# One core, four layers of two transformers: a reordered FFN entry, first batch, softmax maxima and last tail

## The chip, the cores and the metric

The kernel runs on one core of a Trainium2 chip. Its engines each have a queue of their own and meet only through semaphores: TensorE (PE in the profile, its weight loads PEld), VectorE (DVE), ScalarE (ACT), GpSimd (POOL) and SyncE (SP), which issues most of the DMAs. The metric is the time of one execution on the device in microseconds, the median over several runs.

## The reference

Four layers are applied to `x` (4 batches of 512 rows x 512 columns), each added to its input; `ctx` is 4 x 512 x 128:

```python
x = x + L0_xattn(layernorm(x), ctx, ctx)  # RMS norm, rope, 16 query heads on 4 kv heads, causal softmax, w_out
x = x + L0_ffn(layernorm(x))     # silu(x Wg) * (x Wu) Wd, DFF 1376, each with shared and routed rank-8 terms
x = x + L1_xattn(layernorm(x), ctx)
x = x + L1_ffn(layernorm(x))     # 64 experts, top 8, capacity 128 in order of tokens, silu(x Wg) * (x Wu) Wd

def L1_xattn(p, k_v):
    kv = k_v @ W_k.T + b_k
    sim = (p @ kv) @ kv.T * 512 ** -0.5
    sim = (sim - mean(sim)) * rsqrt(var(sim) + 1e-6) * ln_gamma + ln_beta
    return softmax(sim)

def L1_ffn(x):      # T = 2048 tokens
    topk_w, topk_idx = top_k(softmax(x @ router_w.T), 8)
    pos = (cumsum(onehot(topk_idx), axis=0) * onehot).sum(-1) - 1     # place of a token in its expert
    ...             # gather by expert, three products, weighted scatter-add
```

## The kernel before, in words

**Stages.** The four batches run one after another, then all 64 experts. A batch (512 rows = 4 tiles `t` of 128) goes through the attention of layer 0 (`attention`, on every engine a function of that name), its output projection, and the first FFN (`ffn`) in 11 chunks of 128 hidden columns (`NF`). The second cross-attention of a batch and its router, its tail, runs beside the attention of the next batch (`tail` is true there); the tail of the last batch has nothing beside it and is written out alone (`last_tail`, `last_list`, `last_rows`). `keep_clock(bank, n)` issues n spare bf16 products of 512 columns whose result nobody reads. The order on each engine is that of the code; nothing reorders it but the DMA queues.

**Attention.** Four groups `g` of four heads. The scores of a group stand in PSUM in six units (`MAX_UNITS`: tile 3 in two, tile 2 in two, tile 1, tile 0). For each unit VectorE takes the negated row maxima (`maximum(g, i)`, L1446), ScalarE the exponentials with their sums (`exps`, L905), and TensorE turns the probabilities (`turn`, L2120) through three banks used in a ring; VectorE and ScalarE copy them out (`turned`). `stack(g + 1, n)` turns keys (0) and queries (1 to 4) of the next group through the same ring. `normalise(g - 1)` multiplies the last group's output by the inverse sums (L1479), after which GpSimd splits it into a rounded part and a rest (`split_output`). In batch 0 the queries of groups 1 to 3 are still to be made between these (`query_part`, L1310 and L1317, on VectorE).

**Start.** VectorE takes the statistics of the rows, GpSimd the inverse roots; then come keys (`first_keys`), the row shifts (`row_shifts`, fshift) for which ScalarE waits before it makes normed rows (L864), and queries.

**FFN.** Weights come as f32 by DMA (`WRAW`), are rounded to fp32r by ScalarE (`WHI`: `wg_hi`, `wd_hi`) and their rest taken by VectorE (`WLO`: `wg_rest`, `wd_rest`), so that each product is three products. `normed`, `turned`, `turned_rest` make, turn and split the normed rows. Chunk 0's down products (`down_first`, L2448, L2454) use `HH[0]`, `HL[0]`, the two parts of the hidden values, made by GpSimd (L722, L726). Tiles 0 and 1 of its sum go to the banks in which chunk 1's gate and up stood, so they wait for `hid_ready` of chunk 1.

**Last tail.** Output rows (`o1`), their spread under the covariance of the keys (`COV`), weighted (`qv_ready`), give the variance of each similarity row by a product with ones (L2564); GpSimd takes the roots (`power`, L682). `y` scales the similarities, `peak_y` takes maxima, ScalarE exponentials, `x3` the new rows; `top`, `chosen` pick 8 experts, `positions` their places in the lists (a product of the mask with a triangle of ones), to which `TAKEN`, the counts of the earlier batches, is added. `one_hots` writes the list as products of one-hot tiles, `last_slots` masks it (OWN) and `SPREAD_R` brings it into place; IDX then lets the first gather start.

## Time and profile before

| | |
|---|---|
| median of 3 runs | 1270.76 us (1270.14 to 1270.92) |
| profiled execution, whole | 1271.93 us |
| its span, first to last instruction | 1270.1 us |
| mean granted TensorE clock | 0.985 |
| PE busy | 1192.1 us (94%), 6589 products |
| DVE / ACT / POOL busy | 57% / 41% / 38% of the span |
| chain that ended last | PE 77%, DVE 9%, ACT 6%, issue 2%, POOL 2%, DMA 1% |

The span is cut by the profile into stages: the start to 25 us, attention of batch 0 to about 98, FFNs of about 107 us and attentions of about 100 us in turn, the last tail from 875, experts from 918 to 1235, and the last scatters. In a timeline row stand start and length in us, engine, line, operation, out<-in with shapes and count, and in brackets how long the engine had been idle before and what ended it. Starts of neighbouring rows on one engine lie closer than their lengths, since an engine begins an operation before the last is through. In a row of windows stand the stretch and its length, busy time (and instructions) of PE, PEld, DVE, ACT and POOL, the granted TensorE clock as a share of 2.4 GHz, and the DMA share and GB/s. A row of the waits says who waited for whom.

### The profile page before, as it was taken

The numbers are of one execution on the slowest core, as the hardware profiler recorded it, in microseconds if no ns is written. First come the engines' busy times: TensorE is split into PE (matmuls) and PEld (weight loads), VectorE is DVE, ScalarE is ACT, GpSimd is POOL, SyncE is SP. The second block draws the span as 40 slices with busy tenths as digits, with TensorE's granted clock in tenths as the row PEclk, the third lists the DMA queues.
The fourth block names the chain that finished last, engine by engine and source line by source line (L and its number), as shares of the span: only waits on it lengthen the run. The fifth ranks groups of instructions, "written<-read, shape, count | busy, mean of one in ns | idle before, by whom it ended". The sixth has DMA issues, their size and how long they took to land.

```text
span 1270.1 us, 19545 instructions
## 1 busy us (share of the span) xinstructions
PE 1192.1 (94%) x6589; PEld 864.8 (68%) x6589; DVE 724.8 (57%) x1476; ACT 525.2 (41%) x1198; POOL 488.3 (38%) x541
## 2 busy tenths in 40 slices
PE   7998999999999999999999999999899999999980
PEld 4667777667877766777776687777566666666650
DVE  7967565686778578687867866655622222222220
ACT  5864222786322278632247843222332333333220
POOL 1431243462233446123453702121355555565630
PEclk9999999999999999999999999999999999999995
DMA  8012231003233000423300023534789999999847
GB/s 298 4 70 76 103 110 63 2 1 123 90 140 106 33 1 12 148 101 104 128 1 1 34 104 141 217 104 170 256 284 348 353 346 352 354 351 356 205 60 142
DMA packets 45922, 187.04 MB, mean 147 GB/s; under 512 B 6732, under 2 KB 9804, under 8 KB 31380
## 3 DMA queue, kind: packets, MB, share of 16 engines
q1 hardware_dynamic: 30980, 146.18, 30.7%
q0 software_dynamic: 14864, 39.85, 13.7%
q8 instruction: 45, 0.74, 0.2%
q14 instruction: 33, 0.27, 0.1%
HBM read 155.31 MB, written 34.90 MB: 150 GB/s over the span
## 4 chain that ended last, share of the span: by engine, by line
PE 77%; DVE 9%; ACT 6%; issue 2%; POOL 2%; DMA 1%; SPq 0%; DVEq 0%; POOLq 0%; ACTq 0%
PE PS L2613 14%; PE PS L2030 11%; PE PS L2032 11%; PE PS L2031 11%; PE PS L2629 4%; PE PS L2120 3%; ACT P L905 3%; PE PS L2633 3%; PE PS L2139 3%; DVE NM L1446 2%; PE PS L2603 2%; PE PS L2049 2%; PE PS L2430 1%; PE PS L2431 1%; PE PS L2622 1%
## 5 line engine op out<-in xcount | busy, mean ns | idle before, releaser
L2613 PE MATMUL PS<-WE,XGT 128*128 128x384 f32 x512 | 192.7, 499 | 1.5 <-DVE HM L2004 0.8
L722 POOL CAST HH<-HID 128x512 fp32r<-128x512 f32 x44 | 37.5, 852 | 323.9 <-DVE HID L1832 323.9
L1034 ACT ACTIVATE WHI<-WRAW 128x1280 fp32r<-128x1280 f32 x44 | 56.0, 1272 | 244.1 <-DMA WRAW<-in_ffn 244.1
L2030 PE MATMUL PS<-XTH,WHI 128*128 128x512 f32 x352 | 140.7, 400 | 0.0
L905 ACT ACTIVATE P<-PS,NM 128x512 f32<-128x512 f32 (+3 forms) x256 | 131.7, 532 | 15.8 <-DVE NM L1446 15.7
L2032 PE MATMUL PS<-XTH,WLO 128*128 128x512 f32 x352 | 138.2, 393 | 0.0
L2031 PE MATMUL PS<-XTL,WHI 128*128 128x512 f32 x352 | 138.0, 392 | 0.0
L2613 PEld LDWEIGHTS PS<-WE,XGT 128*128 128x128 f32 x512 | 87.1, 190 | 56.7 <-issue 21.5
L2011 DVE COPY HMT<-PS 128x256 f32<-128x256 f32 x64 | 27.2, 425 | 163.9 <-PE PS L2622 163.9
L1446 DVE TENSOR_REDUCE NM<-PS 128x2 f32<-128x1024 f32 (+2 forms) x96 | 98.3, 1040 | 30.7 <-PE PS L2039 30.4
L2120 PE MATMUL PS<-ident,P 128*128 128x128 f32 x640 | 94.2, 279 | 11.8 <-ACT P L905 5.5
L2120 PEld LDWEIGHTS PS<-ident,P 128*128 128x128 f32 x640 | 70.3, 142 | 26.6 <-ACT P L905 16.4
L1176 ACT ACTIVATE SL<-PS 128x192 f32<-128x192 f32 x64 | 21.1, 330 | 152.5 <-PE PS L2613 152.5
L682 POOL TENSOR_TENSOR sm<-sm,mhalf 128x4 f32<-128x4 f32 (+1 forms) x20 | 18.4, 918 | 157.8 <-DVE sm L1365 152.7
L2032 PEld LDWEIGHTS PS<-XTH,WLO 128*128 128x128 f32 x352 | 66.2, 188 | 16.2
L2030 PEld LDWEIGHTS PS<-XTH,WHI 128*128 128x128 f32 x352 | 66.2, 188 | 14.4
L2031 PEld LDWEIGHTS PS<-XTL,WHI 128*128 128x128 f32 x352 | 66.3, 188 | 14.3
L809 POOL DMA_INDIRECT XG<-hx,IDX x56 | 56.4, 1007 | 44.3 <-POOL IDX L806 43.5
L2049 PE MATMUL PS<-KST,QST 128*128 128x512 f32 (+3 forms) x256 | 67.6, 368 | 3.8 <-ACT P L905 3.5
L726 POOL TENSOR_TENSOR HL<-HID,HH 128x512 fp32r<-128x512 f32 x44 | 68.9, 1566 | 3.5
L821 POOL DMA_INDIRECT out<-YE,IDX x32 | 51.0, 1594 | 50.0 <-DVE HM L2004 17.2
L821 POOL DMA_INDIRECT acc<-YE,IDX x32 | 50.8, 1588 | 50.2 <-DMA acc<-YE,IDX 15.9
(341 smaller groups left out, 2737.8 us busy)
## 6 DMA issues: line engine op xcount, KB each, us to landing
WE<-in_we SPq DMA_DIRECT2D x64, 1152.0 KB, 8.1
WRAW<-in_ffn SPq DMA_DIRECT2D x44, 1060.0 KB, 5.0
acc<-HN SPq DMA_DIRECT2D x17, 256.0 KB, 6.4
out<-X SPq DMA_DIRECT2D x4, 1024.0 KB, 4.9
out<-acc POOLq DMA_DIRECT2D x1, 4096.0 KB, 22.9
hx<-HN SPq DMA_DIRECT2D x3, 1152.0 KB, 4.5
XIN<-in_x SPq DMA_DIRECT2D x3, 1024.0 KB, 5.3
CTX<-in_ctx SPq DMA_DIRECT2D x4, 256.0 KB, 2.9
```

Of the source, the lines that this page charges most:

```text
L726: pool.tensor_tensor(HL[slot][:, :], HID[:, :], HH[slot][:, :], ALU.subtract).then_inc(S["hl_ready"], 1)
L809: pool.indirect_dma_start(out=XG[s][:, :], out_offset=None, in_=hx, in_offset=bass.IndirectOffsetOnAxis(ap=IDX1[s][:, 0:1], axis=0),).then ...
L821: pool.indirect_dma_start(out=(out, acc)[s % 2], out_offset=bass.IndirectOffsetOnAxis(ap=IDX1[s][:, 0:1], axis=0), in_=YE[s % NY][:, :], i ...
L905: act.activation(prob(t, n), PS[:, c0:c0 + (t + 1) * P], ACT.Exp, bias=NM[:, c:c + 1], accum_out=SSUM[:, c:c + 1]).then_inc(S["p_ready"], 1)
L1034: act.activation(WHI[slot][:, 0:WD], WRAW[slot][:, 0:WD], ACT.Copy).then_inc(S["wg_hi"], 1)
L1446: dve.tensor_reduce(NM[:, t * HPG + n0:t * HPG + n0 + nh], src, AX, ALU.max, negate=True).then_inc(S["s_max"], 1)
L2030: pe.matmul(dst, a[0], b_[0], start=first, stop=False, **kw)
L2031: pe.matmul(dst, a[0], b_[1], start=False, stop=False, **kw)
L2032: return pe.matmul(dst, a[1], b_[0], start=False, stop=last, **kw)
L2049: pe.matmul(PS[:, a:a + n_keys], QST[n0 + n][:, t * P:(t + 1) * P], KST[:, 0:n_keys], start=(a % 512 == 0), stop=False, skip_group_check=True)
L2120: mm = pe.transpose(bank(bk, c, c + P), prob(t, n0 + n)[:, j * P:(j + 1) * P], ident[:, :])
L2613: mm = pe.matmul(bank(2 + s % 2, 0, 2 * F1), XGT[s % 2][:, k, :], WE[s][:, k * 2 * F1:(k + 1) * 2 * F1], start=(k == 0), stop=(k == KC - 1))
```

## The change

It has ten parts, all in the order or the shape of work; one adds products, one drops spare ones.

1. FFN, every batch: in `down_first` the products with `HL[0]` for ranks and tiles 2 and 3 come ahead of the wait for chunk 1's hidden values.
2. FFN of batch 0: ScalarE makes the first normed rows ahead of key columns and weights, and turns tiles 0 and 1 out ahead of the next weights; VectorE splits both turned tiles before it takes the weights' rest.
3. Start: `row_shifts` comes ahead of the key products and of the wait for the tables; the last add of the other groups' keys (`key_rows`) comes after the first two maxima.
4. Attention, groups 2 and 3: the maximum of unit 4 is taken in two halves with `normalise` between; ScalarE waits for each half. In group 2 the keys are copied out ahead of the last maximum.
5. Batch 0: `query_part(g + 2, 0)` comes after the copy of tile 1's probabilities.
6. Batch 0: `context_T` comes ahead of the last `turn`.
7. Last tail: row variances, their roots and scales in two halves, the products for them in another order.
8. Last tail: `TAKEN` is put under the positions by TensorE (4 products more) and not added by VectorE.
9. Last list: spare products after tiles 1, 2 and 3 go (6 of 8).
10. Last list: OWN is written in two halves, and its products wait for each.

GpSimd's roots of the last tail, and ScalarE's exponentials:

```diff
-            for n in (3, 4, 5):
-                power(B - 1, n)
-            pool.wait_ge(S["norm_out"], 1 + NORMS * B)
+            power(B - 1, 3)
+            power(B - 1, 4, 0, 2)
+            power(B - 1, 5, 2, NT)
+            power(B - 1, 6)
+            pool.wait_ge(S["norm_out"], 1 + NORMS * B + 1)
...
-                act.wait_ge(S["s_max"], 1 + MU * gi + i + 1)
+                act.wait_ge(S["s_max"], 1 + MAXIMA * gi + (i + 2 if i > SPLIT_UNIT else i + 1))
                 for n in range(n0, n0 + nh):
+                    if i == SPLIT_UNIT and n == HPG // 2:
+                        act.wait_ge(S["s_max"], 1 + MAXIMA * gi + i + 2)
                     c0, c = at + (n - n0) * width, t * HPG + n
                     act.activation(prob(t, n), PS[:, c0:c0 + (t + 1) * P], ACT.Exp, bias=NM[:, c:c + 1],
```


ScalarE in `ffn`, where `key_columns` is the copy of KV, `first_weights` the wait for `op_ps` and `wg_hi(0)`, `weights_ahead` `wd_hi(0)` and `wg_hi(1)`:

```diff
+                if b > 0:
+                    key_columns(b)
+                    first_weights()
+                act.wait_ge(S["shift_ready"], 1 + 2 * b + 1)
+                normed(0)
+                normed(1)
+                if b > 0:
+                    weights_ahead()
+                else:
+                    key_columns(b)
+                    first_weights()
+                turned(0)
+                turned(1)
+                if b == 0:
+                    weights_ahead()
+                act.wait_ge(S["shift_ready"], 1 + 2 * b + 2)
+                normed(2)
+                normed(3)
```

VectorE, in this order the start (`key_rows` is the last add of the keys), the attention, the split of turned rows, the last list and the last tail:

```diff
                 assert fstep.n == FIRST["scaled"], fstep.n
+            row_shifts()
             dve.wait_ge(tables_loaded, TABLES_LOADED)
-            dve.wait_ge(S["f_out"], 1 + 1)
-            fstep(first_keys(0, HD, [XN[:, 3, i * P:(i + 1) * P] for i in range(3)], row_shifts))
+            first_spare, rest_spare = [XN[:, 3, i * P:(i + 1) * P] for i in range(3)], (XW, QA, QB)
+            first_keys(0, HD, first_spare)
+            fstep(key_rows(0, HD, first_spare))
             assert fstep.n == FIRST["keys"], fstep.n
             dve.wait_ge(setup_act, QUERY_ROWS)
             first_query(0, 0)
...
                     x2(b, 2)
+                else:
+                    sig(key_rows(HD, CKV, rest_spare), "k_ready", 1)
+                    dve.wait_ge(setup_loaded, SETUP_LOADED)
...
-                    if g > 0:
+                    if g > 1:
+                        maximum(g, 4, 0)
                         normalise(g - 1)
-                    maximum(g, 4)
+                        maximum(g, 4, 1)
+                    else:
+                        if g > 0:
+                            normalise(g - 1)
+                        maximum(g, 4)
                     if g < 2:
...
+                    if g == G - 2:
+                        stack(g + 1, 0, KST)
                     maximum(g, 5)
                     if g < G - 1:
-                        if not sims:
+                        if g < G - 2 and not sims:
                             stack(g + 1, 0, KST)
...
-                    query_part(g + 2, 0)
...
                     turned(g, 1, 0, 2)
+                    query_part(g + 2, 0)
...
                 turned_rest(0)
+                if b == 0:
+                    turned_rest(1)
                 shifts(b, 2, 2, 4)
-                turned_rest(1)
+                if b > 0:
+                    turned_rest(1)
+                else:
+                    wg_rest(0, 0)
...
+                for c0 in (0, SB // 2):
+                    c1 = c0 + SB // 2
+                    dve.tensor_tensor(OWN[:, c0:c1, :].rearrange("p c (g e) -> p g c e", e=GE), parts[:, :, c0:c1, :],
+                                      same[:, :].unsqueeze(1).unsqueeze(2).broadcast_to([P, E1 // GE, c1 - c0, GE]),
+                                      ALU.mult).then_inc(S["own_ready"], 1)
...
+                SPREAD_PS, ROWS_PS, SIM_PS = (1, 3), (2, 6), (4, 5, 7, 8)
+
+                def weigh(half):
+
...
-                    dve.wait_ge(S["sim_ps"], 1 + half + 1)
+                    dve.wait_ge(S["sim_ps"], 1 + SPREAD_PS[half])
                     dve.tensor_tensor(Y[:, NT - 1, sl], bank(6 + half, 0, 2 * P), OT1[:, sl],
                                       ALU.mult).then_inc(S["qv_ready"], 1)
-                dve.wait_ge(S["sim_ps"], 1 + 3)
-                similarity_variances(b, bank(5, 0, NT), step)
...
+                weigh(0)
+                half_variances(0)
+                weigh(1)
+                half_scales(0)
...
                 first = y(0)
+                half_variances(1)
+                peak(0, first)
                 second = y(1)
-                peak(0, first)
+                half_scales(1)
+                peak(1, second)
                 third = y(2)
-                peak(1, second)
                 divide_y(b, 0, 1)
                 x3(0)
...
-                step(dve.tensor_tensor(AT[:, :, :], AT[:, :, :], TAKEN[:, :].unsqueeze(1).broadcast_to([P, NT, E1]),
-                                       ALU.add))
```

TensorE, in this order the attention of batch 0, the last list, the FFN and the last tail:

```diff
+                    if not tail and g == G - 1:
+                        context_T()
...
+                pe.wait_ge(S["pos_taken"], 1 + b)
+                for t in range(NT):
+                    pe.matmul(bank(1, t * E1, (t + 1) * E1), ident[:, :], TAKEN[:, :], start=(t == 0), stop=False,
+                              skip_group_check=True)
                 keep_clock(3, 2)
...
                     one_hots(0, HIGH4[t], LOW4[2][t], False, t == NT - 1).then_inc(S["tile_ps"], 1)
-                    keep_clock(3, 2)
+                    if t == 0:
+                        keep_clock(3, 2)
                 pe.wait_ge(spread_loaded, 32)
-                pe.wait_ge(S["own_ready"], 1 + 1)
                 for c in range(SB):
+                    if c % (SB // 2) == 0:
+                        pe.wait_ge(S["own_ready"], 1 + 2 * c // SB + 1)
                     mm = pe.matmul(bank(2, 0, E1), SPREAD_R[:, c, :], OWN[:, c, :], start=(c == 0), stop=(c == SB - 1))
                 mm.then_inc(S["list_ps"], 1)
                 keep_clock(3, 22)
...
+                    pe.wait_ge(S["hl_ready"], 1 + b * NF + 1)
+                    ranks_down(HL[0], hi)
+                    for t in (2, 3):
+                        rows_down(t, HL[0], hi)
                     pe.wait_ge(S["hid_ready"], 1 + b * NF + 2)
                     for t in (0, 1):
                         rows_down(t, HH[0], hi, lo)
-                    pe.wait_ge(S["hl_ready"], 1 + b * NF + 1)
-                    ranks_down(HL[0], hi)
-                    for t in range(NT):
                         mm = rows_down(t, HL[0], hi)
                     mm.then_inc(S["dn_ps"], 1)
 
...
+                def spread(half):
                     pe.wait_ge(S["o1_sb"], 1 + half + 1)
                     pe.matmul(bank(6 + half, 0, 2 * P), COV[:, :], OT1[:, half * 2 * P:(half + 1) * 2 * P], start=True,
                               stop=True).then_inc(S["sim_ps"], 1)
 
+                def variance_rows(half):
+                    pe.wait_ge(S["qv_ready"], 1 + half + 1)
+                    for t in (2 * half, 2 * half + 1):
+                        mm = pe.matmul(bank(4, t, t + 1), Y[:, NT - 1, t * P:(t + 1) * P], one[:, :], start=True, stop=True)
+                    mm.then_inc(S["sim_ps"], 1)
+
                 def similarity(t):
                     pe.matmul(bank(t), OT1[:, t * P:(t + 1) * P], KVT[:, :], start=True,
                               stop=True).then_inc(S["sim_ps"], 1)
+                pe.wait_ge(S["xT3_sb"], 1 + 2)
+                keys_out(0, 0, KC)
+                pe.wait_ge(S["xT3_sb"], 1 + 4)
+                keys_out(1, 0, 2)
+                spread(0)
+                keys_out(1, 2, KC)
+                variance_rows(0)
+                spread(1)
+                pe.wait_ge(S["gam_ready"], 1 + B)
+                similarity(0)
+                similarity(1)
+                variance_rows(1)
+                similarity(2)
+                similarity(3)
```

TensorE at the entry of the FFN, the down products of chunk 0 (HH and HL the two parts of the hidden values, WHI and WLO those of the weights, 72x512 the ranks), before and after:

```order
L2448 MATMUL PS<-WHI_141,HH_147 128x512
L2448 MATMUL PS<-WLO_143,HH_147 128x512
L2448 MATMUL PS<-WHI_141,HH_147 128x512
L2448 MATMUL PS<-WLO_143,HH_147 128x512
L2448 MATMUL PS<-WHI_141,HH_147 128x512 [waits hid_ready]
L2448 MATMUL PS<-WLO_143,HH_147 128x512
L2448 MATMUL PS<-WHI_141,HH_147 128x512
L2448 MATMUL PS<-WLO_143,HH_147 128x512
L2454 MATMUL PS<-HL_149,WHI_141 72x512 [waits hl_ready]
L2448 MATMUL PS<-WHI_141,HL_149 128x512 x4
L2030 MATMUL PS<-XTH,WHI_141 128x512 [waits sil_ready,wg_lo]
```

```order
L2524 MATMUL PS<-WHI_141,HH_147 128x512
L2524 MATMUL PS<-WLO_143,HH_147 128x512
L2524 MATMUL PS<-WHI_141,HH_147 128x512
L2524 MATMUL PS<-WLO_143,HH_147 128x512
L2530 MATMUL PS<-HL_149,WHI_141 72x512 [waits hl_ready]
L2524 MATMUL PS<-WHI_141,HL_149 128x512 x2
L2524 MATMUL PS<-WHI_141,HH_147 128x512 [waits hid_ready]
L2524 MATMUL PS<-WLO_143,HH_147 128x512
L2524 MATMUL PS<-WHI_141,HL_149 128x512
L2524 MATMUL PS<-WHI_141,HH_147 128x512
L2524 MATMUL PS<-WLO_143,HH_147 128x512
L2524 MATMUL PS<-WHI_141,HL_149 128x512
```

One rank product and two of tile 2 and 3 with HL now stand ahead of the wait for `hid_ready`; three products fewer stand behind it.

VectorE in group 2 of an attention beside a tail (NM the maxima, OT `normalise`, KST the next keys, PT probabilities, nmx the tail's maxima), before and after:

```order
L1455 COPY PT<-PS 128x4x128 [waits ring_ps]
L1413 TENSOR_REDUCE nmx<-XN 128x1 [waits ring_d]
L1479 TENSOR_TENSOR OT<-PS,UN 128x512 [waits out_sb,ring_ps,oT_lo]
L1446 TENSOR_REDUCE NM<-PS 128x4 [waits s_ps] x2
L1460 CAST KST<-PS 128x512 [waits ring_ps]
L1455 COPY PT<-PS 128x3x128 [waits ring_ps] x2
```

```order
L1492 COPY PT<-PS 128x4x128 [waits ring_ps]
L1447 TENSOR_REDUCE nmx<-XN 128x1 [waits ring_d]
L1483 TENSOR_REDUCE NM<-PS 128x2 [waits s_ps]
L1516 TENSOR_TENSOR OT<-PS,UN 128x512 [waits out_sb,ring_ps,oT_lo]
L1483 TENSOR_REDUCE NM<-PS 128x2 [waits s_ps]
L1497 CAST KST<-PS 128x512 [waits ring_ps]
L1483 TENSOR_REDUCE NM<-PS 128x4 [waits s_ps]
```

The maximum of unit 4 has become two rows of 128x2 around OT, and KST has gone ahead of the last maximum.

VectorE in the last tail, from the weighting of the first half to the first new rows (sm the small columns, nmx maxima of y), before and after:

```order
L1899 TENSOR_TENSOR XN<-PS,SCR 128x256 [waits sim_ps,norm_in]
L1899 TENSOR_TENSOR XN<-PS,SCR 128x256 [waits sim_ps]
L1397 TENSOR_TENSOR sm_100<-PS,sm_102 128x4 [waits norm_out,sim_ps]
L1398 TENSOR_TENSOR sm_99<-sm_100,sm_102 128x4 [waits dve_step]
L1399 TENSOR_SCALAR sm_97<-sm_99 128x4 [waits dve_step]
L1404 TENSOR_TENSOR sm_101<-sm_98,sm_102 128x4 [waits norm_out,norm_in]
L1408 SCALAR_TENSOR_TENSOR XN<-PS,sm_101,bet 128x512 [waits sim_ps,dve_step]
L1408 SCALAR_TENSOR_TENSOR XN<-PS,sm_101,bet 128x512 [waits sim_ps]
L1413 TENSOR_REDUCE nmx<-XN 128x1 [waits dve_step]
L1408 SCALAR_TENSOR_TENSOR XN<-PS,sm_101,bet 128x512 [waits sim_ps]
L1413 TENSOR_REDUCE nmx<-XN 128x1 [waits dve_step]
L1418 RECIPROCAL sm_99<-ssum 128x1 [waits e_ready]
```

```order
L1957 TENSOR_TENSOR XN<-PS,SCR 128x256 [waits sim_ps,norm_in]
L1430 TENSOR_TENSOR sm_100<-PS,sm_102 128x2 [waits norm_out,sim_ps]
L1431 TENSOR_TENSOR sm_99<-sm_100,sm_102 128x2 [waits dve_step]
L1432 TENSOR_SCALAR sm_97<-sm_99 128x2 [waits dve_step]
L1957 TENSOR_TENSOR XN<-PS,SCR 128x256 [waits sim_ps,norm_in]
L1438 TENSOR_TENSOR sm_101<-sm_98,sm_102 128x2 [waits norm_out]
L1442 SCALAR_TENSOR_TENSOR XN<-PS,sm_101,bet 128x512 [waits sim_ps,dve_step]
L1430 TENSOR_TENSOR sm_100<-PS,sm_102 128x2 [waits norm_out,sim_ps]
L1431 TENSOR_TENSOR sm_99<-sm_100,sm_102 128x2 [waits dve_step]
L1432 TENSOR_SCALAR sm_97<-sm_99 128x2 [waits dve_step]
L1447 TENSOR_REDUCE nmx<-XN 128x1 [waits dve_step,norm_in]
L1442 SCALAR_TENSOR_TENSOR XN<-PS,sm_101,bet 128x512 [waits sim_ps]
```

The small operations are 128x2 and stand in two blocks, the second of them between the first y and its maximum.

## Rows read from the trace of the kernel before

**Rows 1.** Windows, experts: span, busy us (count) PE PEld DVE ACT POOL, clock, DMA.
```profile
1000.00:1100.00 100.00, 100.00 (x449) 61.90 (x447) 22.30 (x82) 30.98 (x61) 56.03 (x61) 1.00 1.05 355
```

**Rows 2.** Waits: engine, line, releaser, us in total, times, longest.
```profile
PE PS L2448 <- DVE HID L1832: 3.5, 4, 1.0
```

**Rows 3.** Timeline, FFN entry: start, length, engine, operation, [idle before, releaser].
```profile
123.95 2.35 POOL L726 TENSOR_TENSOR HL<-HID,HH 128x512 fp32r<-128x512 f32 x1
...
127.36 0.50 PE L2448 MATMUL PS<-WHI,HH 128*128 128x512 f32 x1 [0.83 <-DVE HID L1832]
...
128.39 0.39 PE L2454 MATMUL PS<-HL,WHI 128*72 128x512 f32 x1
128.62 1.09 PE L2448 MATMUL PS<-WHI,HL 128*128 128x512 f32 x4
```

**Rows 4.** Timeline, attention of batch 1, its third and fourth head group.
```profile
275.06 0.68 DVE L1479 TENSOR_TENSOR OT<-PS,UN 128x512 f32<-128x512 f32 x1
275.29 0.88 ACT L918 ACTIVATE PT<-PS 128x384 f32<-128x384 f32 x2
...
275.65 1.81 DVE L1446 TENSOR_REDUCE NM<-PS 128x4 f32<-128x1024 f32 x2
...
276.90 0.47 ACT L905 ACTIVATE P<-PS,NM 128x256 f32<-128x256 f32 x1 [0.73 <-DVE NM L1446]
...
292.17 0.47 ACT L905 ACTIVATE P<-PS,NM 128x256 f32<-128x256 f32 x1 [0.19 <-DVE NM L1446]
```

**Rows 5.** Timeline, attention of batch 0, where queries are still made.
```profile
35.05 0.68 DVE L1317 TENSOR_TENSOR XN<-X,wq_bc 128x512 f32<-128x512 f32 x1
36.38 0.68 DVE L1455 COPY PT<-PS 128x512 f32<-128x512 f32 x1
...
37.20 0.63 PE L2120 MATMUL PS<-ident,P 128*128 128x128 f32 x4 [0.86 <-DVE PT L1455]
...
37.25 0.43 DVE L1468 COPY RDB<-RD 128x512 f32<-128x512 f32 x1
...
38.45 2.35 DVE L1446 TENSOR_REDUCE NM<-PS 128x2 f32<-128x1024 f32 x2 [0.78 <-PE PS L2039]
...
63.10 0.69 DVE L1446 TENSOR_REDUCE NM<-PS 128x4 f32<-128x512 f32 x1 [0.33 <-PE PS L2039]
...
67.80 2.19 DVE L1468 COPY RDB<-RD 128x512 f32<-128x512 f32 x1
```

**Rows 6.** Chain of waits, attention of batch 0: start, length, what.
```profile
82.40 0.44 PE PS L2230 x4
```

**Rows 7.** Timeline, the start, as far as the last key add.
```profile
12.06 1.65 ACT L864 ACTIVATE X<-XIN,fshift,finv 128x128 f32<-128x128 f32 x4 [8.50 <-DVE fshift L1344]
...
21.16 0.56 DVE L1303 TENSOR_TENSOR KR<-XN 128x384 f32<-128x384 f32 x1
```

**Rows 8.** Timeline, between attention and FFN of batch 0.
```profile
98.24 1.26 ACT L1034 ACTIVATE WHI<-WRAW 128x1280 fp32r<-128x1280 f32 x1
...
100.26 1.36 PE L2393 MATMUL PS<-ident,XN 128*128 128x128 f32 x8 [1.16 <-ACT XN L1044]
...
103.98 0.37 PE L2030 MATMUL PS<-acH,XTH 128*128 128x216 f32 x1 [1.47 <-DVE XTL L1752]
```

**Rows 9.** Timeline, last tail: variances, counts, gates, list.
```profile
883.04 0.16 DVE L1397 TENSOR_TENSOR sm<-PS,sm 128x4 f32<-128x4 f32 x1 [0.70 <-PE PS L2564]
...
884.99 1.41 DVE L1408 SCALAR_TENSOR_TENSOR XN<-PS,sm,bet 128x512 f32<-128x512 f32 x2
...
900.00 0.43 DVE L1958 TENSOR_TENSOR AT<-AT,TAKEN 128x256 f32<-128x256 f32 x1
...
908.50 0.42 DVE L1980 TENSOR_TENSOR HN<-RDB,sm 128x256 f32<-128x256 f32 x1
...
909.67 0.69 DVE L1709 TENSOR_TENSOR OWN<-PS,same 128x512 fp32r<-128x512 f32 x1 [0.75 <-PE PS L2347]
```

**Rows 10.** Windows in the last list.
```profile
906.00:908.00 2.00, 2.00 (x26) 1.45 (x27) 1.97 (x6) 1.02 (x2) 0.00 (x0) 0.50 0.58 218
```

107 lines of the change are left out of this document (51 added, 56 removed).

## The prediction

> **What bounds the kernel now.** I read the table of times and the chain's shares first: TensorE is busy for 94% of the span at a mean granted clock of 0.985, and the chain that ended last runs over it for 77%. So most of the time can be shortened only by fewer or cheaper products, and the change takes none away that matters. Next the windows of the expert stage: in 100 us TensorE is busy for 100 and the clock is full [rows 1]. Nothing of the change touches that stage, which from 918 to 1235 stays as long as it is. What can be won are the places where TensorE stands: 9% of the chain on VectorE and 6% on ScalarE, in the attentions, at the entries of the FFNs and in the last tail. For each part I therefore looked up in the waits who keeps TensorE (or ScalarE, where the exponentials set its pace) waiting, and in the timeline for how long. All sums are made against the profiled execution's own 1271.93 us, which is 1.17 above the median of 1270.76.
>
> **Part 1, `down_first`.** The waits show the stop for chunk 1's hidden values four times, 3.5 us together [rows 2]; in batch 0 it is 0.83 long and ends at 127.36, so it begins at 126.53. HL is complete at 123.95 + 2.35 = 126.30, 0.23 before that. The products that go ahead are one of ranks and two of rows, which start 0.23 apart (128.39, then 128.62), so 0.69 of work [rows 3]. It fits in the 0.83. If it does so every time, the gain is 4 x 0.69 = 2.8; if HL is late by half the stop elsewhere, 1.6. I take **-2.8**, since the margin is measured. Nothing is behind the new wait that was not behind a later one before.
>
> **Part 4, the halved maximum.** In group 2 of an attention beside a tail, `normalise` ran at 275.06 and both maxima from 275.65; ScalarE had copied until 275.29 + 0.88 = 276.17 and stood for 0.73 until 276.90 [rows 4]. A half has 512 elements a row, and a maximum over as many takes 0.69 (at 63.10) [rows 5]. Put in `normalise`'s place it is ready at 275.06 + 0.69 = 275.75, before ScalarE is free, and the 0.73 goes. The second half, after `normalise` (0.6 from start to start), is ready near 276.95; two exponentials of 0.47 end at 277.1. So it isn't late. In group 3 ScalarE stood for 0.19 [rows 4]. Three attentions give 3 x (0.73 + 0.19) = 2.76, less some 0.07 each for the one operation more: **-2.55**. The bounds are -2.8 and 0: zero, if TensorE's ring of three banks and not ScalarE paces that group. `normalise` itself comes 0.6 later; GpSimd, which splits it, is busy for 38% and its result is needed only at the end of the next group. The keys' copy ahead of the last maximum I put at nothing. In batch 0 I find no such stand and count none.
>
> **Parts 5 and 6, queries and `context_T` of batch 0.** Two query operations (from 35.05, 0.7 each) stand ahead of the copy at 36.38, and TensorE stands for 0.86 until 37.20 for that copy. Behind it, the next maximum waits for TensorE's scores with 0.78 idle [rows 5]. With the queries behind the copy TensorE comes up to 0.8 sooner, but the 1.4 of queries then fill that idle time and push on the maximum. So 0 to 0.8 each; I take about the middle, 0.42, twice (groups 0 and 1): **-0.85**. Also in batch 0 the copy of the inverse sums took 2.19 at 67.80 where it took 0.43 at 37.25 [rows 5], with GpSimd at work on queries beside it. With everything a little shifted, some of that may go: **-0.2** (0 to -0.8). `context_T` is on the chain with 0.44 behind the last `turn` [rows 6]; ahead of it TensorE would be waiting anyway: **-0.43**.
>
> The Trainium skill, in "SBUF — State Buffer", section "SBUF: two separate sides", says that VectorE and GpSimd share a port pair as an exclusive lock, and that the loser is blocked for the other's whole operation. The 2.19 us row agrees with that. By that rule a shift that avoids the collision would give the whole 1.8 back and one that makes a new collision would take as much; the sum above goes by its own bounds.
>
> **Part 3, the start.** ScalarE waits for the row shifts and starts the normed rows at 12.06. The last add of the other keys, 0.56 at 21.16, stands right in front of the first maximum [rows 7]. The add goes behind two maxima, where ScalarE has work of four exponentials; of its 0.56 I count 0.5. The shifts come before three key products and the tables, which can bring up to 0.7, but what uses the rows then waits for queries on the same VectorE: 0.2. **-0.7**, between -0.3 and -1.5. The wait for the setup data, moved with the add, has long ended.
>
> **Part 2, entry of the FFN of batch 0.** TensorE stands for 1.16 for the normed rows, which come behind a rounding of weights of 1.26 on ScalarE, and for 1.47 for the rest of the turned rows [rows 8]. Together 2.63. The first goes, as the rows now precede that rounding. The second falls too, since the weights' rest no longer precedes the split. But ScalarE must still round two weights ahead of tile 2's rows, and those become what TensorE waits for. I take **-1.2**, between -0.6 and -1.8.
>
> **Parts 7 to 10, the last tail.** Before, three small operations, a root by GpSimd and a scale lead from 883.04 to `y` at 884.99 [rows 9]. In halves the first `y` starts some 1.5 sooner, but the second half's three small operations, a scale and a wait come between the first y and the first new rows: of 1.5 I keep **-0.25** (+0.4 to -1.0). Adding `TAKEN` cost VectorE 0.43 (0.46 with its start) at 900.00, and TensorE's four products hide behind VectorE: **-0.46**. The spare products go from between tiles. OWN began at 909.67 after 0.75 of idle for TensorE; VectorE's last gate ends at 908.92 [rows 9], and can't be passed: **-0.7**. OWN in halves lets the spread begin half of 0.69 sooner: **-0.35**. Against it stands the clock: in this list it was granted at 0.50 between 906 and 908, with TensorE busy for all of that stretch [rows 10]. Fewer products there leave the last ones at half speed for longer; 16 list products and 8 of the spread, about 1.6 us at full speed, may take half as much again: **+0.8** (0 to +1.6). The parts come to -1.0, between 0 and -1.8.
>
> The Trainium skill, in "TensorE: Matmul & The Clock Gate", section "What's actually happening", takes the throttled clock as the resting state, which only activity releases. By it a list without spare products stays slow and its gain is smaller; the trace agrees as far as 0.50 after a thin stretch goes.
>
> **The sum.** -2.8 - 2.55 - 0.85 - 0.2 - 0.43 - 0.7 - 1.2 - 1.0 = -9.7. 1271.93 - 9.7 = 1262.2, and against the median 1270.76 - 9.7 = **1261.0**. What TensorE-bound stages swallow isn't in it: each of these stands is TensorE's own or ScalarE's in a stage which it paces, so nothing later takes it back, unless it meets one of the rivals. The forecast's own range is 1259 to 1263.
>
> **Rivals.**
> - *The halved maxima and the moved queries pay little.* The ring of three banks, or TensorE's scores, would hold the groups at their pace; for this speaks that VectorE waits for TensorE too (0.78) [rows 5], against it that ScalarE's stand was ended by the maximum. Without three quarters of 3.4: 1263.5.
> - *The clock in the last list doesn't fall.* Then the 0.8 isn't paid: 1260.2. For it: fewer stretches of spare work may only shift the dip. Against it: [rows 10].
> - *More goes than I count*: the 2.19 copy falls to 0.43, the start and the FFN's entry give their outer bounds (0.6, 0.8 and 0.6 more): 1259.
> - *Slower.* With the spare products gone TensorE stays at 1.2 GHz beyond the list into the expert stage, which is TensorE-bound [rows 1]. There each us at half clock costs 0.5. To eat 9.7 it must last 19 us beyond the list, and 24.5 to be over the median by 0.2%; at 28 us it is 1261.0 + 14 = 1275, the price I set. Against it: the clock came back while the list still ran.
> - *Nothing comes of it*: every stand is replaced by another that ended just behind it (HL late, tile 2's rows late, the gates late). Then all at their poor bounds: 1.6 + 0 + 0 + 0 + 0.4 + 0.3 + 0.6 + 0 = 2.9, 1267.9; within 0.2% with little more.
>
> **How the numbers follow.** Forecast 0.60; little from maxima 0.16; clock stays 0.09; more 0.06; slower 0.03; nothing 0.06. A measurement of this kernel tells 0.2% from no change, which is 2.5 us: below 1268.2 is faster. The "nothing" case lies at that bound, 0.02 of it below and 0.04 above; with the first four that makes faster 0.93, same 0.04, slower 0.03. The range must leave out no more than 2 in 10: 1257.5, which holds the "more" case and 1.5 beyond, to 1265.0, which holds the first rival and its spread.
>
> **What would show each step.** In the new profile: TensorE's stand at chunk 1's hidden values is under 0.25 in each FFN (part 1). The exponential of tile 1 in group 2 has no idle for the maximum ahead of it, and the groups are shorter by 0.7 (part 4). No 0.86 stand for the copy in batch 0 (5). The maximum of the start right behind the last key product (3). The two stands of 1.16 and 1.47 are replaced by one for tile 2's normed rows (2). OWN begins within 0.1 of the gates, and the clock in the list is 0.50 for some 3 to 5 us (9, 10). The experts take the same time as before. The forecast is wrong if the attentions of batches 1 to 3 each keep their length, or if the granted clock is low after the list.

## The result and the profile after

| | before | after |
|---|---|---|
| median of 4 runs each | 1270.84 us (1270.14 to 1271.27) | 1261.53 us (1261.30 to 1263.98) |
| ratio, 95% interval | | 0.9932 (0.9918 to 0.9946) |
| profiled execution, its span | 1271.93 us, 1270.1 us | 1261.52 us, 1259.7 us |
| PE busy | 94% | 95% |

The kernel became 9.3 us faster by the medians, and the forecast was 1261.0. The two profiled executions lie 10.4 us apart, as that of before is 1.1 above its median. The page of the changed kernel, in its part on busy time:

```profile
PE 1194.1 (95%) x6591; PEld 865.0 (69%) x6591; DVE 727.2 (58%) x1488; ACT 525.0 (42%) x1198; POOL 488.9 (39%) x542
```

No engine's busy time fell by more than 0.2 us (TensorE had 1192.1 before). What went is waiting. To see where, I took instructions that both kernels have, and noted by how much each starts earlier in the trace after:

| instruction | starts earlier by | gained since the row above |
|---|---|---|
| VectorE: second query part of group 1, batch 0 (start of the kernel) | 0.65 | 0.65 |
| first maxima of groups 1 and 2, batch 0 | 1.27, 1.80 | 0.6 and 0.5 |
| first maximum of group 3, batch 0 | 1.81 | 0.0 |
| TensorE: output products, batch 0 | 2.32 | 0.5 |
| its first gate product, batch 0 | 3.59 | 1.27 |
| first maxima of batch 1; first normed rows' rest after it | 4.29, 5.35 | 0.70 and 1.06 |
| the same two of batch 2 | 6.21, 7.23 | 0.86 and 1.02 |
| the same two of batch 3 | 7.82, 8.87 | 0.59 and 1.05 |
| VectorE: first output sum of the last FFN | 9.34 | 0.47 |
| new rows of the last tail (x3) | 9.79 | 0.45 |
| positions, after the counts | 10.25 | 0.46 |
| OWN | 10.97 | 0.72 |
| the list's indices (IDX) | 11.31 | 0.34 |
| first expert's rows, turned | 10.39 | **-0.92** |
| last scatter | 10.40 | 0.0 |

Up to the last list, stages that no edit touches have the same length in all traces to within a few hundredths, with two exceptions: the start, and FFNs in which weights land late. So a gain between two rows belongs to the edits that lie between them. The 0.65 of the start is not the edits' alone. Of the 1.09 by which the first query is earlier, 0.44 is there already in the statistics of `x` (fvar at 9.36, before at 9.80), because the input landed earlier in this trace; the new order gives the other 0.65 (from fvar to fshift 1.41, before 2.07). Against it, TensorE's clock rose later in this trace, its opening products that nobody reads ended 1.2 later, and the first maximum then waited 0.60 for TensorE.

The entry of an FFN, timeline of the changed kernel (it answers to [rows 3]): the rank product with HL and two row products now stand ahead of the product at 123.78 that waits for the hidden values. No stand is left in TensorE's rows.

```profile
122.56 0.39 PE L2524 MATMUL PS<-WLO,HH 128*128 128x512 f32 x1
122.78 0.44 PE L2530 MATMUL PS<-HL,WHI 128*72 128x512 f32 x1
123.03 0.69 DVE L1887 TENSOR_TENSOR HID<-SIL,PS 128x512 f32<-128x512 f32 x1
123.06 0.63 PE L2524 MATMUL PS<-WHI,HL 128*128 128x512 f32 x2
123.78 0.50 PE L2524 MATMUL PS<-WHI,HH 128*128 128x512 f32 x1
```

Group 2 beside a tail, timeline of the changed kernel (to [rows 4]): two half maxima of 0.68 around `normalise`, and the exponential at 271.75 follows ScalarE's copies without a bracket, so without a stand. In batch 0 the turn that stood for 0.86 [rows 5] has no stand either (last row).

```profile
270.77 0.68 DVE L1483 TENSOR_REDUCE NM<-PS 128x2 f32<-128x512 f32 x1
...
271.01 0.88 ACT L923 ACTIVATE PT<-PS 128x384 f32<-128x384 f32 x2
...
271.37 0.68 DVE L1516 TENSOR_TENSOR OT<-PS,UN 128x512 f32<-128x512 f32 x1
...
271.75 0.50 ACT L910 ACTIVATE P<-PS,NM 128x256 f32<-128x256 f32 x1
271.97 0.68 DVE L1483 TENSOR_REDUCE NM<-PS 128x2 f32<-128x512 f32 x1
```

```profile
35.49 0.60 PE L2188 MATMUL PS<-ident,P 128*128 128x128 f32 x4
```

Batch 0, timeline (to [rows 5] and [rows 8]): the copy of the inverse sums is as slow as it was, beside a GpSimd operation of 2.04. At the FFN's entry stands of 1.07, 0.18 and 0.44 have taken the place of 1.16 and 1.47, 0.94 less; the first eight turns of normed rows also take 1.04 in place of 1.36.

```profile
65.87 2.04 POOL L764 TENSOR_TENSOR acL<-ac_raw,acH 128x864 fp32r<-128x864 f32 x1
65.95 2.24 DVE L1505 COPY RDB<-RD 128x512 f32<-128x512 f32 x1
...
99.62 0.37 PE L2098 MATMUL PS<-acH,XTH 128*128 128x216 f32 x1 [1.07 <-DVE XTL L1801]
...
101.40 0.66 PE L2469 MATMUL PS<-ident,XN 128*128 128x128 f32 x4 [0.18 <-ACT XN L1049]
...
104.26 0.37 PE L2098 MATMUL PS<-acH,XTH 128*128 128x216 f32 x1 [0.44 <-DVE XTL L1801]
```

The end of the last list, timeline of the changed kernel: the 22 spare products behind the spread start at 900.16 and take 6.61 us. The first expert's rows have landed before 905.60, where VectorE copies from them, and TensorE turns them only at 906.61, with no idle before: it was still at the spare products.

```profile
898.70 0.75 DVE L1758 TENSOR_TENSOR OWN<-PS,same 128x256 fp32r<-128x256 f32 x2
...
899.27 0.94 PE L2461 MATMUL PS<-OWN,SPREAD_R 128*128 128x64 f32 x7 [1.56 <-DVE OWN L1758]
...
900.16 6.61 PE L2130 MATMUL PS<-mask_qk,identb 128*128 128x512 bf16 x22
...
905.60 0.15 DVE L2066 COPY WC<-XG 128x1 f32<-128x1 f32 x1 [4.70 <-DMA XG<-hx,IDX]
...
906.61 0.60 PE L2694 MATMUL PS<-ident,XG 128*128 128x128 f32 x4
```

Its windows (the clock is the third number from the right) show why. The clock is 1.00 in the whole list, where it was 0.50 before [rows 10], and falls behind it.

```profile
892.00:894.00 2.00, 1.80 (x22) 0.92 (x21) 2.00 (x5) 2.00 (x6) 2.00 (x2) 1.00 0.96 375
...
898.00:900.00 2.00, 0.73 (x7) 0.76 (x7) 1.35 (x4) 0.00 (x0) 0.00 (x0) 1.00 0.21 52
900.00:902.00 2.00, 2.00 (x10) 0.97 (x10) 0.51 (x2) 0.00 (x0) 0.17 (x1) 0.80 0.13 29
902.00:904.00 2.00, 2.00 (x6) 0.74 (x5) 0.00 (x0) 0.00 (x0) 1.70 (x2) 0.50 0.22 30
```

### The profile page after: what moved, and what is told of

It reads as the page before. It is cut to its first block, busy times and chain, and to the rows that moved or that the text cites. A ratio compares the mean times of both kernels' runs of the same rounds, so it can differ in the third digit from the quotient of the medians.

```text
span 1259.7 us, 19573 instructions
## 1 busy us (share of the span) xinstructions
PE 1194.1 (95%) x6591; PEld 865.0 (69%) x6591; DVE 727.2 (58%) x1488; ACT 525.0 (42%) x1198; POOL 488.9 (39%) x542
## 4 chain that ended last, share of the span: by engine, by line
PE 77%; DVE 9%; ACT 7%; issue 3%; POOL 2%; DMA 0%; DVEq 0%; POOLq 0%
PE PS L2704 14%; PE PS L2098 11%; PE PS L2100 11%; PE PS L2099 11%; PE PS L2720 4%; ACT P L910 4%; PE PS L2724 3%; PE PS L2188 3%; PE PS L2207 2%; DVE NM L1483 2%; PE PS L2694 2%; PE PS L2506 1%; PE PS L2507 1%; PE PS L2117 1%; PE PS L2713 1%
## 5 line engine op out<-in xcount | busy, mean ns | idle before, releaser
L1483 DVE TENSOR_REDUCE NM<-PS 128x2 f32<-128x1024 f32 (+4 forms) x104 | 99.6, 971 | 29.9 <-PE PS L2107 29.2
```

The lines of the kernel that those rows point to most:

```text
L1483: dve.tensor_reduce(NM[:, t * HPG + n0:t * HPG + n0 + nh], src, AX, ALU.max, negate=True).then_inc(S["s_max"], 2 if i == SPLIT_UNIT and pa ...
```

## The experiments

All start from the changed kernel. "Trace" numbers are differences of starts between traces, taken inside the stage concerned, since other things move too: the landing of the first input and the clock at the start shift a whole trace by up to 0.6 us, and in the third FFN late weights added 1.0 to 1.3 in three of the traces (16 spare products, keys ahead, VectorE's entry undone) and up to 0.35 in others. In four traces (old down products, keys ahead, the copy behind both maxima, ScalarE's entry undone) the low clock in the last list lasted twice as long as in the changed kernel, which cost another 0.6 to 1.4 between the spread and the first expert's turns. Medians are of 4 runs (the last of 5), beside a kernel before at 1270.95 to 1271.58. The changed kernel's 1261.53 stands beside 1270.84.

Parts 1, 2, 4, 8 and 9, and half of part 3, were undone in a run. Parts 5, 6, 7 and 10 were not: what they gained is read from their places in the table above.

### The parts that gained as forecast

**Down products in the old order.**

```diff
-                    pe.wait_ge(S["hl_ready"], 1 + b * NF + 1)
-                    ranks_down(HL[0], hi)
-                    for t in (2, 3):
-                        rows_down(t, HL[0], hi)
                     pe.wait_ge(S["hid_ready"], 1 + b * NF + 2)
                     for t in (0, 1):
                         rows_down(t, HH[0], hi, lo)
-                        mm = rows_down(t, HL[0], hi)
+                    pe.wait_ge(S["hl_ready"], 1 + b * NF + 1)
+                    ranks_down(HL[0], hi)
+                    for t in range(NT):
+                        mm = rows_down(t, HL[0], hi)
```

> The changed kernel with the down products of chunk 0 in their old order (products with HL behind the wait for chunk 1's hidden values). Theory A: the stand of 0.5 to 0.9 is back in all four FFNs, 2.4 to 2.8 in all, the time is about 1264.1. Rival B (a later stand in the FFN takes most of it back): under 1 us slower.

1264.08 us (1263.43 to 1266.22), 2.5 above the changed kernel. In the trace the stand is back four times at 0.83, the first of them here:

```profile
124.03 0.50 PE L2524 MATMUL PS<-WHI,HH 128*128 128x512 f32 x1 [0.83 <-DVE HID L1887]
```

The four FFNs are 0.69, 0.71, 0.58 and 0.69 longer, 2.7 in all. Theory A.

**Whole maxima, keys still copied early.**

```diff
-                    if g > 1:
-                        maximum(g, 4, 0)
-                        normalise(g - 1)
-                        maximum(g, 4, 1)
-                    else:
-                        if g > 0:
-                            normalise(g - 1)
-                        maximum(g, 4)
+                    if g > 0:
+                        normalise(g - 1)
+                    maximum(g, 4)
```

> The changed kernel with the maximum of unit 4 whole again in groups 2 and 3 (normalise ahead of it), but with the keys of group 3 still copied out ahead of the last maximum. Theory A (the halves carry the gain of the attentions): ScalarE stands again for about 0.7 in group 2 and 0.2 in group 3 in three batches, the time goes up by 2.7 to 3.1, to about 1264.4. Rival B (the keys' copy carries half of it): up by 1.5 only. Batch 0: no change by A.

1264.88 us (1264.57 to 1265.20). ScalarE's stand is back:

```profile
271.59 1.22 DVE L1483 TENSOR_REDUCE NM<-PS 128x4 f32<-128x1024 f32 x1
...
272.85 0.47 ACT L910 ACTIVATE P<-PS,NM 128x256 f32<-128x256 f32 x1 [0.73 <-DVE NM L1483]
```

In the trace the attentions of batches 1 to 3 are 1.05 to 1.08 longer each. That is all that these three attentions gained, so the halves carry it and the keys' earlier copy nothing: theory A. The attention of batch 0, where theory A had no change, is longer by 0.16. So of the 0.5 that its end gained, 0.16 are the halves' and 0.35 are left for `context_T`.

### The entry of the first FFN: two orders that need each other

ScalarE's order undone:

```diff
-                if b > 0:
-                    key_columns(b)
-                    first_weights()
+                key_columns(b)
+                first_weights()
                 act.wait_ge(S["shift_ready"], 1 + 2 * b + 1)
                 normed(0)
                 normed(1)
-                if b > 0:
-                    weights_ahead()
-                else:
-                    key_columns(b)
-                    first_weights()
+                weights_ahead()
                 turned(0)
                 turned(1)
-                if b == 0:
-                    weights_ahead()
```

> The changed kernel with ScalarE's order at the entry of the FFN of batch 0 as before (key columns and weights ahead of the first normed rows, the next weights ahead of the turned rows), VectorE's order left changed. Theory A (ScalarE's order is what TensorE waited for): the stand of 1.2 us for normed rows is back, the FFN's products start 1.0 to 1.3 us later, time 1262.7. Rival B (VectorE's split ahead of the weights' rest gave most): less than 0.5 us.

VectorE's order undone:

```diff
-                if b > 0:
-                    wg_rest(0, 0)
+                wg_rest(0, 0)
                 turned_rest(0)
-                if b == 0:
-                    turned_rest(1)
                 shifts(b, 2, 2, 4)
-                if b > 0:
-                    turned_rest(1)
-                else:
-                    wg_rest(0, 0)
+                turned_rest(1)
```

> The changed kernel with VectorE's order at the entry of the FFN of batch 0 as before (the weights' rest ahead of the turned rows' rest), ScalarE's order left changed. With ScalarE's order undone alone the FFN came 2.0 us later. Theory A (both matter, for VectorE then takes the weights' rest, 1.7 us, ahead of the rest of the first turned rows): the FFN's products of all tiles come 0.8 to 1.5 us later. Rival B (ScalarE's order alone decides): under 0.3 us.

1264.92 us and 1264.87 us. Inside the stage the first costs 2.02 (another 1.4 went in its last list, by the clock) and the second 1.22 (1.2 went to late weights). Beside the kernel before, where both orders are old, the whole step is worth 1.27. Both runs say theory A, the first with twice its price. So VectorE's new order with ScalarE's old one is 0.8 *slower* than both old, ScalarE's new with VectorE's old is as slow as both old, and only both new gain. TensorE's rows show it, first with ScalarE's order old, then with VectorE's:

```profile
97.79 1.36 PE L2462 MATMUL PS<-ident,XN 128*128 128x128 f32 x8 [1.15 <-ACT XN L1049]
...
101.52 0.37 PE L2091 MATMUL PS<-acH,XTH 128*128 128x216 f32 x1 [1.47 <-DVE XTL L1794]
...
102.42 1.52 ACT L1049 ACTIVATE XN<-X,sm,sm 128x512 f32<-128x512 f32 x2 [1.27 <-DVE sm L1762]
```

```profile
98.66 1.22 DVE L1809 TENSOR_TENSOR WLO<-WRAW,WHI 128x1024 fp32r<-128x1024 f32 x1
...
101.18 0.37 PE L2092 MATMUL PS<-acH,XTH 128*128 128x216 f32 x1 [3.06 <-DVE XTL L1801]
```

In the first, VectorE splits both turned tiles before it makes the shifts, and its split waits for ScalarE, so ScalarE stands for 1.27 at the normed rows of tile 2 until VectorE's small columns (sm) come; that is what both old orders didn't have. In the second the normed rows' stand is gone, but the 1.7 us of weights' rest stand ahead of the split, and one stand of 3.06 holds what were two.

### The start

```diff
             first_keys(HD, CKV, rest_spare)
+            sig(key_rows(HD, CKV, rest_spare), "k_ready", 1)
...
-                    sig(key_rows(HD, CKV, rest_spare), "k_ready", 1)
```

> The changed kernel with the last add of the other keys (0.56 us) ahead of the first maximum again, everything else of the start as changed. In the changed kernel the maximum waits 0.60 us for TensorE there. Theory A (the earlier shifts gave the whole gain of the start; the add fits into that wait, and behind the maxima it costs its 0.56): the first maximum stays at 20.6 and the rest of batch 0 comes 0.3 to 0.5 us earlier, time 1261.1. Rival B (moving the add was worth its 0.56): 0.5 us slower.

1262.76 us (1260.31 to 1264.42), which tells nothing at this size. I compare it with the run of six spare products below, as the clock stays at 1.00 in the start of both. Rows of the one with the add ahead, then of the other (QR the last query step, NM the first maxima):

```profile
15.64 0.69 DVE L1355 TENSOR_TENSOR QR<-XN 128x512 f32<-128x512 f32 x1
...
20.55 0.56 DVE L1335 TENSOR_TENSOR KR<-XN 128x384 f32<-128x384 f32 x1
...
21.14 2.36 DVE L1484 TENSOR_REDUCE NM<-PS 128x2 f32<-128x1024 f32 x2
...
24.74 0.95 DVE L1484 TENSOR_REDUCE NM<-PS 128x2 f32<-128x768 f32 x1
```

```profile
15.54 0.69 DVE L1355 TENSOR_TENSOR QR<-XN 128x512 f32<-128x512 f32 x1
...
20.47 2.35 DVE L1483 TENSOR_REDUCE NM<-PS 128x2 f32<-128x1024 f32 x2
22.74 0.55 DVE L1335 TENSOR_TENSOR KR<-XN 128x384 f32<-128x384 f32 x1
...
24.66 0.95 DVE L1483 TENSOR_REDUCE NM<-PS 128x2 f32<-128x768 f32 x1
```

From QR the first maximum is 5.50 and 4.93 away, so the add does stand in front of it; the third maximum is 9.10 and 9.12 away, and so it stays in group 1. Neither theory: the moved add gains 0.57 at one maximum and gives it back before the third. So the start's gain is the earlier row shifts' alone. From the statistics (fvar) to the third maximum it is 15.66 in the trace before and 14.92 to 14.94 in the seven traces of the new shifts in which TensorE isn't late, the one with the add ahead among them: 0.73, free of when the input lands.

### The copy that GpSimd holds

Only the copy moved, first behind both maxima of group 3, then between them. The reciprocal in front of it stays, since ScalarE would else write the next sums before they are read; so moving both has no time.

```diff
                 gstep(dve.reciprocal(RD[:, :], SSUM[:, :]))
+                if not late:
+                    divisor_rows()
...
                     maximum(g + 1, 0)
+                    if late:
+                        divisor_rows()      # between
                     maximum(g + 1, 1)
```

> On the changed kernel, in the attention of batch 0 only the copy of the inverse sums of group 2 (2.24 us beside a GpSimd operation of 2.04 us) comes behind the first two maxima of group 3; its reciprocal stays. Theory A (the copy is held by the GpSimd operation beside it, a maximum out of PSUM in its place is not): the maximum starts about 1.8 us earlier, the attention of batch 0 gets 1.2 to 1.8 us shorter, the time is about 1260. Rival B (whatever VectorE operation stands there is held until GpSimd is through): the first maximum itself takes over 3 us, nothing is gained. Rival C (the copy now meets the next GpSimd operation of 4.55 us): it takes up to 4 us, and the time is the same or 1 us worse.

> On the changed kernel, the copy of the inverse sums of group 2 in batch 0 stands between the first two maxima of group 3, so after the GpSimd operation of 2.04 us and ahead of the next of 4.55 us. Theory A (the copy is held exactly as long as a GpSimd operation runs, and the maximum isn't): the first maximum starts 0.85 us earlier, as when the copy came behind both; the copy takes 0.43 us, the attention of batch 0 is 0.5 to 0.9 us shorter, time 1260.8. Rival B (the copy still meets the long operation): over 3 us slower, as with the copy behind both maxima.

Behind both: 1264.86 us, 3.3 slower, rival C. The maximum came 0.87 earlier (then it waited for TensorE), but the copy started 0.36 behind the next GpSimd operation and ended 0.27 behind its end:

```profile
67.04 2.35 DVE L1483 TENSOR_REDUCE NM<-PS 128x2 f32<-128x1024 f32 x2 [1.32 <-PE PS L2115]
68.95 4.55 POOL L764 TENSOR_TENSOR woL<-wo_raw,woH 128x2048 fp32r<-128x2048 f32 x1 [1.25 <-ACT woH L893]
69.31 4.46 DVE L1510 COPY RDB<-RD 128x512 f32<-128x512 f32 x1
```

Not all of the 3.3 is VectorE's time. Behind the copy TensorE stood for 2.60, and its clock fell to 0.50 from about 75 to 78, as it did there in no other trace:

```profile
76.00:78.00 2.00, 2.00 (x12) 1.91 (x10) 0.70 (x2) 1.49 (x4) 0.00 (x0) 0.50 0.03 8
```

Between them, in the gap that GpSimd leaves:

```profile
65.46 2.06 POOL L764 TENSOR_TENSOR acL<-ac_raw,acH 128x864 fp32r<-128x864 f32 x1
...
66.84 1.23 DVE L1483 TENSOR_REDUCE NM<-PS 128x2 f32<-128x1024 f32 x1 [1.32 <-PE PS L2115]
67.98 0.42 DVE L1510 COPY RDB<-RD 128x512 f32<-128x512 f32 x1
68.31 1.22 DVE L1483 TENSOR_REDUCE NM<-PS 128x2 f32<-128x1024 f32 x1
```

The copy takes 0.42, and the maxima at 66.84 and 68.31 their usual 1.23 and 1.22, though each overlaps a GpSimd operation by 0.7 to 0.8. Of 0.87 at the maximum 0.4 is left at the end of the attention. The median is 1261.93 (1261.31 to 1264.17), no gain that it can tell: in this trace 0.3 went again in the last list, as it did in all three traces with the copy moved. So it is the copy from memory to memory that is held, for the whole of GpSimd's operation, and not the maximum out of PSUM. Theory A holds for the copy; the attention gained less than it said. This agrees with the Trainium skill, "SBUF — State Buffer", section "SBUF: two separate sides", which lets the loser of the shared port pair block fully, for copies in a two-port mode among others.

### The last list and TensorE's clock

**16 spare products behind the spread in place of 22.**

```diff
-                keep_clock(3, 22)
+                keep_clock(3, 16)
```

> On the changed kernel, 16 spare products instead of 22 stand between the spread of the last list and the first expert's turns. Theory A (at half clock these spare products end about 1 us behind the landing of the first gather, and the first expert's turns queue behind them): the first turned rows come 0.9 us earlier after the list's indices, the kernel is 0.8 to 1.0 us faster than the changed one, about 1260.6. Rival B (the gather itself sets the first expert's start): 0. Rival C (fewer spare products leave the clock low into the experts): slower by up to 1 us, and the granted clock beyond 906 us is under 1.

1261.12 us (1259.89 to 1262.03), no difference that the medians can tell. From the indices to the first expert's rows it takes 0.90 less, as theory A says, but the clock fell earlier in this trace and reached the spread (1.52 in place of about 1.0), which took 0.5 back:

```profile
900.29 1.52 PE L2461 MATMUL PS<-OWN,SPREAD_R 128*128 128x64 f32 x8 [1.56 <-DVE OWN L1758]
901.62 4.85 PE L2130 MATMUL PS<-mask_qk,identb 128*128 128x512 bf16 x16
...
907.13 0.66 PE L2694 MATMUL PS<-ident,XG 128*128 128x128 f32 x4 [0.66 <-DMA XG<-hx,IDX]
```

**The spare products between tiles back.**

```diff
-                    if t == 0:
-                        keep_clock(3, 2)
+                    keep_clock(3, 2)
```

> The changed kernel with the two spare products behind each tile of the last list again. Theory A (they stood in TensorE's way): the masked list (OWN) starts about 0.7 us later after the router's mask, and the list's indices come that much later. [...] Time 1262.2. Rival B (the spare products keep the clock up and pay for themselves): the granted clock stays 1.00 from 895 to 910, the first expert starts as early as now or earlier, the time 1261.0.

1260.30 us (1259.72 to 1260.45), 1.2 *less* than the changed kernel. OWN starts no later (0.02 by the trace), the granted clock is 1.00 through the list and behind it, the 22 spare products take 4.93, and TensorE waits for the gather:

```profile
900.04 4.93 PE L2130 MATMUL PS<-mask_qk,identb 128*128 128x512 bf16 x22
...
905.50 0.66 PE L2693 MATMUL PS<-ident,XG 128*128 128x128 f32 x4 [0.53 <-DMA XG<-hx,IDX]
```

So part 9 of the change, taken by itself, cost about 0.9 and gained nothing. Rival B. The early fall of the clock (last section), which this trace lacks, isn't the reason: the stretch in which it lies takes the same time with it and without it, to 0.01.

**The same, and VectorE adds the counts again.**

```diff
+                step(dve.tensor_tensor(AT[:, :, :], AT[:, :, :], TAKEN[:, :].unsqueeze(1).broadcast_to([P, NT, E1]),
+                                       ALU.add))
...
-                for t in range(NT):
-                    pe.matmul(bank(1, t * E1, (t + 1) * E1), ident[:, :], TAKEN[:, :], start=(t == 0), stop=False,
-                              skip_group_check=True)
...
```

> The changed kernel with the counts (TAKEN) added by VectorE again, TensorE's four products for them gone, and the two spare products behind each tile back. Beside the run that had only the spare products back (1260.3, the clock at 1.00 all through the list), Theory A (what lets the clock fall is the thin stretch that the add lengthens and the four products don't fill): the clock falls to 0.50 within or behind the list, OWN starts 0.5 to 1.2 us later, time 1261.5 to 1262. Rival B (the counts cost VectorE their 0.46 and nothing of the clock): OWN 0.46 later, the clock stays at 1.00, time 1260.8.

1262.00 us (1261.21 to 1262.41), 1.7 more than with the spare products back alone. OWN starts 1.16 later: 0.46 for the add, and 0.7 as the clock falls inside the list again, as in the kernel before. TensorE had been busy for 0.64 of the 2 us from 892 (1.79 with the spare products back alone):

```profile
892.00:894.00 2.00, 0.64 (x5) 0.15 (x4) 1.95 (x6) 1.80 (x3) 1.68 (x2) 1.00 0.96 374
...
896.00:898.00 2.00, 1.65 (x18) 1.10 (x18) 2.00 (x6) 1.45 (x3) 0.00 (x0) 0.50 0.77 279
```

Theory A. The other traces agree: in the twelve with the counts on TensorE OWN starts 0.45 behind the start of the last gate, whatever the clock did; in the kernel before it was 1.17 and here 1.00.

**Six spare products where TensorE waits for OWN.**

```diff
+                    if t == NT - 1:
+                        keep_clock(3, 6)
```

> The changed kernel with six spare products between the last tile of the list and the wait for OWN, where TensorE stands for 1.56 us. Theory A (they fill idle time and hold the clock): OWN's products start no later, the clock doesn't fall behind the spread or falls later and shorter, the first expert's turned rows come 0.5 to 0.9 us sooner, time 1260.8. Rival B (the stretch that lets the clock fall lies earlier, between 894 and 898): the dip stays, no gain. Rival C (six of them take longer than the stand): the spread starts up to 0.3 us later.

1259.94 us (1259.71 to 1261.01). The stand of 1.56 is 0.27, OWN and the spread are where they were, the clock doesn't fall, and the first expert starts 0.95 sooner. Theory A.

```profile
897.59 1.46 PE L2130 MATMUL PS<-mask_qk,identb 128*128 128x512 bf16 x6
...
899.31 0.94 PE L2463 MATMUL PS<-OWN,SPREAD_R 128*128 128x64 f32 x7 [0.27 <-DVE OWN L1758]
...
900.20 4.93 PE L2130 MATMUL PS<-mask_qk,identb 128*128 128x512 bf16 x22
```

**Both edits that gained** (these six, and the copy between the maxima).

> The changed kernel with the two edits that gained in traces of their own: six spare products ahead of the wait for OWN (0.95 us), and the copy of the inverse sums of group 2 in batch 0 between the first two maxima of group 3 (0.4 us). Theory A (they lie in different stages and add): the first expert starts 1.3 us earlier than in the changed kernel, the time is about 1259.8, the ratio to the kernel before about 0.991. Rival B (the shifted times let the clock fall in the list after all, as it did a little earlier or later in other runs): 1260.8 or more, the granted clock 0.50 somewhere between 895 and 906.

1260.37 us (1260.26 to 1260.83), ratio to the kernel before 0.9915 (0.9902 to 0.9929). It is 1.2 faster than the changed kernel by the medians, but no faster than six spare products alone. In the trace the copy gained 0.34 and 0.3 went in the list, as in the copy's own run. The clock held, so neither theory: rival B's fall didn't come, and the sum of theory A didn't either. Why VectorE loses 0.3 there when code far ahead is moved stays open.

## Why the prediction was right, and where its terms were off

| term | forecast | traces |
|---|---|---|
| down products | -2.8 | -2.6 (undone: 2.7) |
| halved maxima | -2.55 | -3.1, and -0.16 in batch 0 |
| queries; copy of sums; `context_T` | -0.85; -0.2; -0.43 | -1.1; 0; -0.35 |
| start | -0.7 | -0.65 (the order alone: -0.73) |
| entry of the first FFN | -1.2 | -1.27 |
| variance in halves | -0.25 | -0.45 |
| counts | -0.46 | -0.46 |
| OWN earlier; OWN in halves | -0.7; -0.35 | -0.72; -0.34 |
| clock | +0.8 | +0.92 |
| sum | -9.7 | -10.4 |

The forecast was 1261.0 and the median is 1261.53, with the four largest terms (down products, maxima, entry, queries) found at their places, so the number isn't luck as a whole. Three things in it are luck: the errors of the terms cancel to 0.7, in the start two wrong prices add up to the right sum, and the clock's 0.8 was paid elsewhere than I had put it.

- **Down products.** Right by place and price: 0.69 of products went into a stand of 0.83. Theirs is the cleanest step, since the margin of HL (0.23) was in the rows.
- **Maxima.** Right by place, 0.7 too small. I took 0.73 and 0.19 a batch and then some off; it gave 0.80 in group 2 and 0.25 in and behind group 3, and 0.16 in batch 0, where I had counted none. No ring of banks took it back, so the first rival fell.
- **Queries.** 0.55 each and not 0.42: nearer the whole 0.6 by which the copy could start earlier. The GpSimd collision did not go by "a little shift", since it moved along with everything; it took a place of its own in GpSimd's gap to end it. I also misread what GpSimd does beside the copy: it is the rest of a weight (acL), not the queries.
- **Start.** Right sum, wrong reason: I gave 0.5 to the moved add and 0.2 to the shifts. The run with the add put back shows 0 for the add, and the shifts are worth 0.73.
- **Entry.** The size was right. What was to be left isn't: I expected one stand, for tile 2's normed rows behind ScalarE's rounding. That one is 0.18, and the larger two, 1.07 and 0.44, are for VectorE's split. Nor did I say that neither half of the step works alone.
- **Last list.** The steps have their sizes, but two of their causes are wrong. I gave OWN's 0.7 to the dropped spare products. The runs show that they cost nothing at OWN; the 0.7 came with the counts on TensorE (1.16 with the add's 0.46), for with them the clock never fell earlier than 1.5 ahead of OWN, and without them it fell over 4 ahead. And I set the 0.8 of the clock inside the list, on the list's own products. It fell behind the list, and was paid through 22 spare products at half clock that the first expert's rows had to wait for. That is what dropping the spare products really did. A low clock behind the list was one of my own two signs of a wrong forecast; it came, but short of the experts, and cost 0.9.

The Trainium skill, in "TensorE: Matmul & The Clock Gate", section "What's actually happening", says that activity releases the throttle. Three runs agree with it (the spare products back, six ahead of OWN, and both edits): filled with idle work, the list keeps 1.00. What I drew from it, a slow list without the spare products, didn't come: in the changed kernel the list ran at 1.00.

## What to carry to other kernels

Products that nobody reads are judged at the place where they end, too: six spare products that fill a known wait cost nothing, and 22 of them at half clock held up the work queued behind them by 0.9 us. Where two engines feed one stage, try their orders in all four combinations, since here each alone gained nothing or lost. And a copy from memory to memory on VectorE is best put into a gap of GpSimd; in one place it took 0.42 us, in the next 4.46. The 0.4 that this won in the attention is too small for the medians here.
